# A transformer block on one core: the opening in a new order, and three PSUM banks in rotation

## The reference, cut to what matters

```python
# B, T, C = 4, 256, 256; fside serves as key and value of both recurrences
def bi_wkv(r, k, v, w, u, time_emb):
    tf = sigmoid(sum(time_emb)); decay = exp(-exp(w)) * (0.5 + 0.5 * tf)
    ek = exp(min(k, 30)); ekv = ek * v
    # scans over T, forward and backward: a = a * decay + ekv, b = b * decay + ek
    euk = exp(min(u + k, 30))
    num = nf + nb - ekv + euk * v
    den = df + db - ek + euk
    return sigmoid(r) * (num / max(den, 1e-8)) * (0.8 + 0.2 * tf)

x = x + attention(bi_wkv(x, fside, fside, ...))   # 16 query heads of 128, 4 key/value heads, causal, q and k normalized
x = x + ffn(bi_wkv(x, fside, fside, ...))
# ffn, 8 groups g of 8 experts, I = 176:
xg = x + soft_g @ mask_up_w[g].T                  # soft: softmax over the top 8 of 64 router scores, by group
a  = silu(xg @ gate_proj_w[g].T) * (xg @ up_proj_w[g].T)
y += scalar_g * (a @ down_proj_w[g].T)
```

## Time and profile before

| what | value |
|---|---|
| time, median of 3 runs | 416.12 us (415.92 to 416.34) |
| the profiled execution: time, span | 415.53 us, 413.7 us |
| busy in the span: TensorE, VectorE, ScalarE, GpSimd | 367.5, 326.3, 275.6, 218.2 us |
| instructions | 6407 |
| chain that ended last | TensorE 62%, VectorE 19%, ScalarE 12%, issue 5% |

### The profile page before, as it was taken

The page is one execution under the profiler, slowest core; times in us unless marked ns, Lnnn a source line. Parts: engine busy times, 40 slices in busy tenths (PEclk is TensorE's granted clock), DMA queues, the critical chain, the costliest instruction groups (busy, mean ns, idle before and its releaser), DMA issues.

```text
span 413.7 us, 6407 instructions
## 1 busy us (share of the span) xinstructions
PE 367.5 (89%) x1952; PEld 295.1 (71%) x1952; DVE 326.3 (79%) x759; ACT 275.6 (67%) x673; POOL 218.2 (53%) x230
## 2 busy tenths in 40 slices
PE   0099869899999799898999997999899999999995
PEld 0098656688878667687787776687687878788884
DVE  8999789988988997599999889476566787575543
ACT  6447789798789497796978879784274424443321
POOL 6260614278524868133693121563269756898831
PEclk9999999999999999999999999999999999999999
DMA  7725300112100304001021000110065533374121
GB/s 213 302 77 194 106 0 5 47 56 100 52 0 2 103 0 154 1 2 51 2 101 40 1 2 0 38 46 33 2 188 158 151 104 102 96 226 152 52 76 51
DMA packets 14209, 31.92 MB, mean 77 GB/s; under 512 B 1872, under 2 KB 4432, under 8 KB 14176
## 3 DMA queue, kind: packets, MB, share of 16 engines
q1 hardware_dynamic: 13888, 31.38, 23.8%
q10 hardware_dynamic: 288, 0.14, 0.1%
HBM read 30.43 MB, written 1.08 MB: 76 GB/s over the span
## 4 chain that ended last, share of the span: by engine, by line
PE 62%; DVE 19%; ACT 12%; issue 5%; POOLq 0%; POOL 0%; DVEq 0%; ACTq 0%
PE ov L1223 7%; PE sc L1201 6%; PE acc L1126 5%; PE tr L1152 5%; PE acc L1128 5%; PE acc L1127 5%; PE proj L1140 4%; PE proj L1144 3%; PE proj L1141 3%; ACT PR L625 3%; PE tr L1127 2%; PE tr L1126 2%; PE tr L1128 2%; PE sc L1126 2%; PE sc L1128 2%
## 5 line engine op out<-in xcount | busy, mean ns | idle before, releaser
L598 POOL TENSOR_TENSOR WL<-stage,WH 128x256 fp32r<-128x256 f32 x142 | 125.4, 912 | 75.6 <-ACT WH L664 75.6
L612 POOL TENSOR_TENSOR PR<-PR,RI 128x512 f32<-128x512 f32 x48 | 53.6, 1133 | 80.8 <-DVE RI L1072 80.8
L1140 PE MATMUL proj<-WH,RH 128*128 128x512 f32 x96 | 42.6, 443 | 32.0 <-DVE RL L923 19.9
L1126 PE MATMUL acc<-OH,WH 128*128 128x256 f32 (+1 forms) x172 | 55.0, 320 | 2.9 <-DVE OL L1084 2.2
L625 ACT ACTIVATE PR<-PR,MX 128x128 f32<-128x128 f32 (+1 forms) x128 | 56.6, 455 | 0.0
L1128 PE MATMUL acc<-OH,WL 128*128 128x256 f32 (+1 forms) x172 | 53.5, 311 | 0.0
L1127 PE MATMUL acc<-OL,WH 128*128 128x256 f32 (+1 forms) x172 | 53.4, 311 | 0.0
L1201 PEld LDWEIGHTS sc<-kT,QT 128*128 128x128 f32 x256 | 41.0, 191 | 15.8 <-issue 12.8
L1223 PE MATMUL ov<-PTS,V 128*128 128x512 f32 x96 | 46.6, 594 | 1.1 <-DVE OL L1084 1.1
L1201 PE MATMUL sc<-kT,QT 128*128 128x128 f32 (+1 forms) x256 | 47.2, 327 | 0.0
L1140 PEld LDWEIGHTS proj<-WH,RH 128*128 128x128 f32 x96 | 18.4, 192 | 38.6 <-issue 36.2
(11 more groups left out here) (160 smaller groups left out, 870.5 us busy)
## 6 DMA issues: line engine op xcount, KB each, us to landing
stage<-in_ffn SPq DMA_DIRECT2D x22, 384.0 KB, 3.3
stage<-in_wq SPq DMA_DIRECT2D x8, 512.0 KB, 3.6
stage<-in_wo SPq DMA_DIRECT2D x8, 512.0 KB, 3.4
SBC<-group_scalars SPq DMA_DIRECT2D x8, 256.0 KB, 3.6
PR<-in_tables SPq DMA_DIRECT2D x4, 352.0 KB, 7.5
fT<-in_fT SPq DMA_DIRECT2D x4, 256.0 KB, 4.2
xT<-in_xT SPq DMA_DIRECT2D x4, 256.0 KB, 4.2
stage<-in_wk SPq DMA_DIRECT2D x2, 512.0 KB, 4.9
```

Of the source, the lines that this page charges most:

```text
L598: i = pool.tensor_tensor(lo[:, c:c + 256], src[:, c:c + 256], hi[:, c:c + 256].bitcast(F32), ALU.subtract)
L612: pool.tensor_tensor(pr, pr, RI[:, m % 4, hs[0]:hs[0] + nh].rearrange("p (h o) -> p h o", o=1).broadcast_to([P, nh, 512 // nh]), ALU.mult) ...
L1126: mm(o, lh, rh, start=first, stop=False, skip_group_check=True)
L1140: mm(proj[:], rh[ch], wh[ch], start=ch == 0, stop=False, skip_group_check=True)
```

## The change

- **Order of loads.** SP issues fside 0, the mask's source, table 0, the constants, tables 1 and 2, wk, tables 3 and 4, fside 1, table 5, the gate weights, wq 0, tables 6 and 7, and only then x of sequences 1 to 3. x of sequence 0 goes through ScalarE's queue. Tables 6 and 7 have places of their own, in kT.
- **Order of the opening on TensorE.** Tables R0 to R6 and the sums stand ahead of the first projection.
- **Sums on TensorE.** For sequence 0 of layer 1 forward, backward and bonus terms are added by matmuls with the identity into `sc0`: three for the denominator, three for the numerator.
- **Gate.** exp(-x) by ScalarE (step `ex`), min and + 1 by GpSimd, and VectorE multiplies it into the denominator together with the maximum; the separate product with the tanh gate and the second activation table load at the start are gone.
- **Mask.** `bmask` becomes one copy with a padded layout that the matmul reads at an offset.
- **Tables placed by GpSimd.** ScalarE copies `acc` out twice at full height (an exact and a rounded copy of 352 columns), GpSimd makes the rest and puts four groups into EX.
- **Banks.** `proj`, `tr0`, `tr1` become three banks in rotation over K1, A, V, K3, B, D and the router; E keeps a bank of its own.
- **Projections** take both products with RH first and wait for RL behind them. **Y** takes the four products with OH first and waits for OL behind them.
- The orders of the lists and the places of background steps change.

```diff
@@ START @@
-    "PE": [("split", "K", 0), ("small",), ("split", "Q", 0), ("K1", 0, 0), ("R", 0), ("K1", 0, 1), ("R", 1),
-           ("R", 2), ("R", 3), ("R", 4), ("R", 5), ("K3", 0, 0), ("K3", 0, 1)],
+    "PE": [("R", 0), ("sum", 0, 0), ("R", 1), ("R", 2), ("sum", 0, 1), ("sum", 0, 2), ("R", 3),
+           ("R", 4), ("R", 5), ("R", 6), ("K1", 0, 0), ("R", 7), ("split", "K", 0), ("small",),
+           ("split", "Q", 0), ("K1", 0, 1), ("K3", 0, 0), ("K3", 0, 1)],
-    "ACT": [("wkv", 1, 0, 1), ("tanh", 0), ("tanh", 1), ("tanh", 2), ("tanh", 3), ("logs",), ("wkv", 1, 0, 6),
...
+    "ACT": [("wkv", 1, 0, 1), ("ex", 0), ("wkv", 1, 0, 6), ("split", "K", 0), ("wkv", 1, 0, 7), ("ex", 1), ("small",),
+            ("wkv", 1, 1, 1), ("split", "Q", 0), ("K1", 0, 0), ("K1", 0, 1), ("K2", 0, 0), ("wkv", 1, 1, 6), ("K3", 0, 0),
+            ("K3", 0, 1), ("wkv", 1, 1, 7)],
+    "POOL": [("ex", 0), ("split", "K", 0), ("small",), ("ex", 1)],
@@ make_plan @@
-    for i, st in ((2, ("split", "V", 0)), (0, ("R", 6)), (0, ("R", 7)), (0, ("table", 0)), (3, ("table", 1)),
+    for i, st in ((1, ("split", "V", 0)), (1, ("table", 0)), (7, ("table", 1)),
...
+    for b, i in enumerate([1, 1, 3, 6]):
+        put(bg, i, ("ex", b))
@@ banks @@
+            k = OUT_BANK if st[0] == "E" else n % (2 if late else OUT_BANK)
+            bank[st], old[st] = k, holder.get(k)
+            holder[k] = st
+            n += st[0] != "E"
@@ GpSimd @@
-            linked(pool.memset(V[:], 0.0))
+            linked(pool.memset(VX[:], 0.0))
+            pool.wait_ge(s["mup_in"], 16)
+            o = VX[:, 96:96 + CH * G * P].rearrange("p (i y) -> p i y", y=P)[:, :, 0:3 * GS].rearrange("p i (o e) -> p i o e", o=3)
+            pool.tensor_copy(o, mup[:, :, :].rearrange("p c n -> p (c n)").rearrange("p (i o e) -> p i o e", o=1, e=GS).broadcast_to([P, CH * G, 3, GS])).then_inc(s["bmask_ready"], 1)
...
+                    pool.tensor_scalar(gate1(b), gate1(b), GATE_CAP, 1.0, ALU.min, ALU.add).then_inc(s["gate_ready"], 1)
...
+                    linked(pool.tensor_scalar(SX[:, 0, part], SX[:, 0, part].bitcast(F32), table_rest, None, ALU.mult))
+                    for g in range(4 * h, 4 * h + 4):
...
+                        i = pool.tensor_tensor(EX[rows, h, :, table_col(g):table_col(g) + FI], hi, x, ALU.add)
@@ VectorE, wkv @@
+                    if summed(L, b):
+                        dve.wait_ge(s["sum_ready"], 2 * b + 1)
+                        dve.wait_ge(s["gate_ready"], b + 1)
+                        done(v.scalar_tensor_tensor(out=DF, in0=sum_bank(b, 0), scalar=1e-8, in1=gate1(b), op0=ALU.max, op1=ALU.mult))
+                        return
@@ TensorE @@
+                elif st[0] == "sum":
+                    _, b, k = st
+                    n0 = wkv_before(ND, 1, b)
+                    if k == 1:
+                        pe.wait_ge(s["wkv_dve"], n0 + 8)
+                    for x, n, kind in ((DF, 3, 0), (DB, 4, 0), (EUX[:], 5, 0), (NF, 6, 1), (NB, 7, 1), (EU[:], 9, 2)):
+                        if kind == k:
+                            pe.wait_ge(s["wkv_dve"], n0 + n)
+                            i = mm(sum_bank(b, min(k, 1)), ident, x, start=n in (3, 6), stop=n in (5, 9), skip_group_check=True)
+                    if k != 1:
+                        i.then_inc(s["sum_ready"], 1)
@@ Y @@
-                    pe.wait_ge(s["a_lo"], f + 1)
+                    pe.wait_ge(s["a_hi"], f + 1)
...
                     for mc in range(2):
-                        w = wblock(wst, 512 + P * mc, 512 + P * mc + P)
-                        i = three(acc[mc][:], w[0], w[1], OH[:, sl], OL[:, sl], m == 0, m == FT - 1)
+                        mm(acc[mc][:], w[mc][0], OH[:, sl], start=m == 0, stop=False, skip_group_check=True)
+                        mm(acc[mc][:], w[mc][1], OH[:, sl], start=False, stop=False, skip_group_check=True)
+                    pe.wait_ge(s["a_lo"], f + 1)
+                    for mc in range(2):
+                        i = mm(acc[mc][:], w[mc][0], OL[:, sl], start=False, stop=m == FT - 1, skip_group_check=True)
```

354 lines of the change are left out of this document (194 added, 160 removed), and 12 rows, old and new, of the table ORDERS.

## The result

The changed kernel takes **422.15 us** (median of 5 runs, 419.99 to 422.39) where the kernel before takes 415.92 (5 runs, 415.66 to 416.34): ratio 1.0140, 95% interval 1.0125 to 1.0154. It is 1.4% slower; 407.9 was forecast, with the range from 402.0 to 413.2. Kernels with the new opening spread more from one execution to the next than the kernel before, by up to 6 us where it spreads by up to 1.5, so a single trace of theirs can lie well off its median.

What follows compares the result with a forecast made beforehand. VectorE was taken to bound the kernel ahead of 76 us and TensorE from there on. The terms -1.6 - 3.0 - 3.0 - 0.6 = -8.2 gave 407.9 us on the median's scale, own range 404.6 to 411.2, wider range 402 to 413.2.

Steps and rivals of the forecast that it cites:

- The order of the steps and the stage loads otherwise change which work lies where, and no row prices that; nothing: Whole kernel: the remaining changes in step order and stage loads were booked at nothing.
- F waits for ScalarE's copies alone: Attention output projection F: nobody waits for GpSimd's table placing before the routing; nothing taken.
- Opening, -1.6: Up to 45 us: 1.2 late, less 2.35 for table placements and 0.43 for the fused gate on VectorE, gives -1.6 us.
- 45 to 76, -3.0: From 45 to 76 us: VectorE loses 2.35 + 0.43 us and projections stop waiting for ScalarE; -3.0 us.
- 76 to 300, -3.0: From 76 to 300 us: half of 6.0 us of bank waits come back as data waits; -3.0 us (0 to -6.0).
- the rotation couples what was apart: Rival, 0.08: each of 32 projections waits 0.3 us more for a turn's bank, 9.6 us; +1.4, 417.5 us.
- Tables on GpSimd, nothing: GpSimd's placing takes 4.8 to 10 us per table on an engine with idle time; no cost taken.
- GpSimd's placements slow VectorE: Rival, 0.08, up to 76 us: placing lengthens VectorE's steps, about 3 us of the gain go back; 410.9 us.
- Mask copy: Opening: one copy of 384 elements taken at 2.5 us, so the mask stands at 7.9 (6.4 to 11.3).
- the rival by elements: Rival, 0.10, opening: mask copy goes by elements, mask at 11.3, 3.4 late; +1.4 at 45 us, 410.9 us.
- Tail, -0.6: Last tile: four matmuls go ahead of OL and the first half completes sooner; -0.6 us.

Runs made afterwards that it cites:

- the warmed run: Eight more fp32 matmuls of 512 columns, result unread, in TensorE's wait ahead of K3, added to the mended order: 415.22 us.
- the mended order: Changed kernel with table half 1 copied and placed two background steps earlier and query weights 6 and 7 split 2 and 3 steps ahead: 414.45 us.
- the old order: Changed kernel with the step lists and places of the kernel before from the first item on: 416.69 us.
- sums 0.4: Sums of sequence 0 back on VectorE, against the mended order: 414.02 us.
- first scores -0.4: ScalarE's two copies of the first query projection ahead of the rounded result of sequence 1 and the cast of query weights 1, against the mended order: 414.83 us.
- placing 0.5: GpSimd's placing of the tables left out but for eight columns, against the mended order: 413.99 us.
- gates -1.6: Minimum and plus one of the gate on VectorE instead of GpSimd, against the mended order: 416.01 us.
- items 17 and 19: GpSimd places the table halves at these items, against the mended order with ScalarE's copies of the first query projection ahead: 416.54 us.
- items 11 and 13: GpSimd places the table halves at these items instead of 1 and 5, against the mended order: 418.58 us.
- the kernel with the old opening: The kernel before with only the three banks in rotation and the down projection's OL products last: 411.07 us.

## Why the prediction was wrong

**The step that failed** is the sentence "The order of the steps and the stage loads otherwise change which work lies where, and no row prices that; nothing", together with "F waits for ScalarE's copies alone", which was read as a cover and was the wait. Each queue is in order. That ScalarE's copy of table half 1 had moved from item 3 to 7, behind a step that waits for VectorE, and the splits 6 and 7 from two and three items ahead to one, stood in the diff, and rows of before could have priced a part: the split's chain is one cast (1.05 in the changed kernel) and four subtractions (2.79 alone), and its cast stands behind a whole item of ScalarE's work. The runs give 7.7 us for the two, against a forecast of 0.

**Opening, -1.6.** Wrong in sign: +5.6 in the order of before, with gates and placing in it. The times of its steps were near: R0 at 7.42 (7.9), K1 (0,0) at 23.70 (23.9), K3 at 35.36 (34.8), the last multiply at 20.0 (19.7), the first scan of sequence 1 at 23.34 (22.95), RL at 40.73 (39.9). R0 was near by luck: the mask, for which 7.9 was worked out, stood at 6.6, and R0 waited for table 0, which was put at 6.0 and came at 7.4. Half rate behind the 7.4 us wait ahead of K3 was not in the sum; the warmed run says it costs nothing in the mended order. The wrong inference was that being 0.65 us earlier with RL (1.6 was forecast) is a gain of the kernel. Behind it the other engines' queues count: in the changed kernel ScalarE went to 28.3 of 31 us from 45 to 76, GpSimd to 18.9, and F (0) came 2.1 late. In the old order the loss lies between 41 and 66 us; which part causes it stays open. What was tried was tried in the mended order: sums 0.4, first scores -0.4, placing 0.5 and the warmed gap -0.8, none of them clear of noise, and gates -1.6. The gates are the one part shown to be a gain.

**45 to 76, -3.0, and 76 to 300, -3.0.** The bank waits did go, and nearly all of them. What they give back is 4.0 us in the old order, where 6.0 were forecast together with VectorE's freed time, and 10.1 in the new one. Behind F (0) the rotation with OL last gains 3.0 us in the old order, the -3.0 of the forecast. From F (0) to F (15) the mended version gains 4.7. The mechanism was right; its size depends on the order. The rival "the rotation couples what was apart" did not decide: projections wait 2.9 us in all for turns to be emptied, where it needed 9.6.

**Tables on GpSimd, nothing.** 5.2 us each (4.8 to 10 was the estimate), worth 0.5 us at the place chosen (within the noise), 1.7 more at items 17 and 19, and 4.1 more at items 11 and 13, where the queue is full. The rival "GpSimd's placements slow VectorE" had the right mechanism (scans of 1.97 us for 1.21 beside the placing; the steps of 1.2 to 1.5 us for 0.68 ran beside GpSimd's other work); at the place chosen at most a sixth of its 3 us shows.

**Mask copy.** 0.84 us for 384 elements against 5.85 for eight of 48: so here the cost went with the number of instructions. 2.5 was taken; the rival by elements is out. The gate step on GpSimd was put at 1.0 and takes 1.9 to 2.4.

**Tail, -0.6.** 0.4 in the trace of the changed kernel (from the last GB matmul at 409.46 to the end of the span at 418.2, 8.7 us, where it was 9.15), 0.4 and 0.9 in medians. Right, as far as these can tell.

The books in medians: 415.9 - 4.0 (rotation) - 0.9 (OL last) + 5.6 (opening) + 7.7 (two places) - 2.2 (rest of the order) = 422.1, measured 422.15. They close because the terms are differences of a chain of kernels, and the 2.2 is the remainder; that they close proves nothing.

## What to carry to other kernels

When a change rewrites the order of in-order queues, list for each moved step what now stands ahead of it and what that waits for, and price it; copies of 0.9 us behind a wait of 3.4 cost 4 us. A change of several parts should be tried by parts on the old order: here rotation and OL last alone beat the whole by 11 us. A moment reached earlier on the engine that bounds was worth nothing here, where the engines behind it had got more to do; look at what they do next before booking it as a gain.

## What was not expected of the hardware

- GpSimd's TENSOR_SCALAR of 128x512 takes 1.93 to 2.38 us (with two operations, minimum and add), a TENSOR_SCALAR of the same size on VectorE 0.43 (at 20.11 us in the changed kernel); the copy of 384 elements takes 0.84. The Trainium skill puts GpSimd's two-input steps at about twice VectorE's time and says "1-input is roughly line-rate" (GPSIMD Engine Reference, section Engine selection). Here a one-input step takes four to six times VectorE's 0.43, and the measurement decides.
- TensorE's first matmuls run at half rate for a length that differs from one execution to the next, and with the sums on TensorE this reaches VectorE: its first step behind the sums starts at 12.39 us in one trace and at 14.44 in another, with the same opening:

```profile
9.26 1.39 PE L1260 MATMUL sc<-F,const 128*128 128x512 f32 x2
10.48 1.02 PE L1260 MATMUL sc<-B,const 128*128 128x512 f32 x2
```
```profile
9.87 1.92 PE L1260 MATMUL sc<-F,const 128*128 128x512 f32 x2
11.57 1.91 PE L1260 MATMUL sc<-B,const 128*128 128x512 f32 x2
```

  The first is the version with the first scores ahead (413.02 us), the second that with the tables at items 17 and 19 (417.15). Of the 2.05 us some 0.6 are table 0, which came at 6.75 and 7.36; the rest is the longer half rate. A single pair of such traces therefore decides nothing below 2 us.
- After idle waits of 3.7 us (at 85) and 3.1 us (at 237) the matmuls came at the 1.2 GHz level for 3 to 4 us, though TensorE had been 89% busy from 45 to 76 and 88% from 200 to 235 us. In the kernel with the old opening, whose longest wait behind its first matmul is 2.2 us, every stretch reads 1.00. Shorter waits can do it too: with the tables at items 11 and 13 a wait of 2.06 us (up to 221.90) was followed by a granted clock of 0.72 from 222 to 228. And one wait goes both ways: in the old order TensorE stands 2.33 us for GpSimd's normalization in two traces; behind it three pairs of matmuls of 512 columns take 0.71, 0.62 and 0.62 us in one (from 100.51), and 0.76, 1.05 and 1.05 in the other (from 101.32). The slower executions of these kernels are those with the lower granted clock (414.98 us at 0.992 and 420.76 at 0.971 for table 1 two items earlier); which causes which is not shown.
